# A recurrent four-layer kernel on one Trainium2 core: the second layer's input product moved from whole-array matmuls into column tiles of the recurrence's PSUM, and the order of each tile's work rewritten

## The reference

```python
# layer 0: modulated dense layer (ys and d depend on the batch row only)
x = x + einsum('bsi,io->bso', x * ys[:, None, :], weight) * d[:, None, :]
# layer 1: tanh RNN over the 128 steps
h = tanh(h @ Wh + (x @ Wx + b))        # x = x + all h
# layer 2: per row a dense layer, base + a rank-8 product A B made from cond
x = x + (x + x @ (base + A B))
# layer 3: LSTM over the 128 steps
a = x @ Wx + b + h @ Wh                # 512 -> 2048: gates i, f, o, g
c = sigmoid(f) * c + sigmoid(i) * tanh(g); h = sigmoid(o) * tanh(c)   # x = x + all h
```

## Time and profile before

| what | value |
|---|---|
| median of 3 runs | 1139.91 us (1139.41 to 1141.58) |
| the profiled execution | 1140.8 us, its span 1139.0 us |
| instructions | 57838, of them 26364 matmuls |
| TensorE busy | 97% of the span |
| VectorE, ScalarE, GpSimd busy | 80%, 37%, 5% |
| granted TensorE clock, mean | 0.995 |

### The profile page before, as it was taken

How to read it: one execution, slowest core, us unless ns; L and a number is a source line. 1 busy time by engine, 2 the same in 40 slices (tenths; PEclk the granted TensorE clock), 3 DMA queues, 4 the chain that set the end, 5 groups by cost and what they waited for, 6 DMA issues and landing times.

```text
span 1139.0 us, 57838 instructions
## 1 busy us (share of the span) xinstructions
PE 1099.2 (97%) x26364; PEld 744.4 (65%) x26364; DVE 908.3 (80%) x2726; ACT 426.1 (37%) x1034; POOL 55.2 (5%) x75
## 2 busy tenths in 40 slices
PE   5779999999999999999999999999999999999997
PEld 3446656766766676667666666766666676667587
DVE  7898888888878888887788888888888887887766
ACT  6784333333333333333333333333333333333332
POOL 0000000000000000000000000000000000000000
PEclk9899999999999999999999999999999999999999
DMA  9991000000000000000000000000000000000000
GB/s 338 404 369 40 22 22 3 22 22 22 22 22 21 4 22 21 22 22 22 22 14 11 22 22 22 22 22 19 6 22 22 22 22 21 13 3 13 12 14 22
DMA packets 24613, 51.45 MB, mean 45 GB/s; under 512 B 4160, under 2 KB 4288, under 8 KB 23344
## 3 DMA queue, kind: packets, MB, share of 16 engines
q1 hardware_dynamic: 23936, 47.49, 11.8%
q10 hardware_dynamic: 432, 0.26, 0.1%
HBM read 39.36 MB, written 8.39 MB: 42 GB/s over the span
## 4 chain that ended last, share of the span: by engine, by line
PE 83%; DVE 8%; DMA 3%; ACT 2%; issue 1%; SPq 1%; ACTq 0%; DVEq 0%
PE ps_gates L1543 52%; PE ps_l L1474 13%; PE ps_x L1474 7%; PE ps_rnn L1591 7%; DMA ring<-in_hw 3%; PE ps_lr L1474 2%; PE ps_l L1543 2%; DVE gates_ring L1103 1%; SPq L403 1%; PE ps_z L1512 1%; DVE rnn_pre L928 1%; PE ps_gates L1443 1%; DMA rows<-in_ln_b 1%; DVE late L1133 0%; ACT rnn_h L522 0%
## 5 line engine op out<-in xcount | busy, mean ns | idle before, releaser
L1543 PE MATMUL ps_gates<-big,rows 128*32 128x512 f16 (+1 forms) x6144 | 344.4, 372 | 2.1 <-DVE gates_ring L1103 1.3
L1543 PE MATMUL ps_gates<-big,lstm_h 128*32 128x512 f16 (+1 forms) x6144 | 343.8, 372 | 2.1 <-DVE lstm_h L1136 2.0
L1543 PEld LDWEIGHTS ps_gates<-big,rows 128*32 128x32 f16 x6144 | 163.6, 97 | 162.2 <-DVE gates_ring L1103 10.2
L1543 PEld LDWEIGHTS ps_gates<-big,lstm_h 128*32 128x32 f16 x6144 | 160.4, 97 | 148.0 <-DVE lstm_h L1136 3.6
L657 ACT ACTIVATE gates_ring<-gates_ring 128x256 f32<-128x256 f32 x128 | 53.4, 417 | 284.0 <-DVE gates_ring L1103 284.0
L1103 DVE SCALAR_TENSOR_TENSOR gates_ring<-ps_gates,tile_un,rows 128x256 f32<-128x256 f32 x248 | 108.8, 479 | 37.6 <-PE ps_gates L1543 37.6
L1591 PE MATMUL ps_rnn<-wh_hi,rnn_h 128*32 128x128 f16 x4096 | 103.4, 221 | 1.3 <-ACT rnn_h L522 0.7
L1133 DVE SCALAR_TENSOR_TENSOR late<-gates_ring,tile_g,cell_tanh 128x128 f16<-128x128 f32 x127 | 44.7, 352 | 60.2 <-ACT cell_tanh L666 60.2
L1591 PEld LDWEIGHTS ps_rnn<-wh_hi,rnn_h 128*32 128x32 f16 x4096 | 72.0, 97 | 26.3 <-issue 4.4
L1474 PE MATMUL ps_l<-xs,w_hi 128*128 128x128 f16 x1024 | 79.5, 221 | 1.6 <-DVE xs L837 1.6
L1474 PE MATMUL ps_l<-x,wx_hi 128*128 128x128 f16 x1024 | 78.1, 219 | 1.5 <-DVE x L837 1.5
(11 more groups left out here) (201 smaller groups left out, 1596.0 us busy)
## 6 DMA issues: line engine op xcount, KB each, us to landing
ring<-in_hw SPq DMA_DIRECT2D x16, 1024.0 KB, 15.0
xT_sb<-in_xT SPq DMA_DIRECT2D x32, 256.0 KB, 2.8
outT<-late SPq DMA_DIRECT2D x32, 256.0 KB, 2.0
big<-in_wx SPq DMA_DIRECT2D x5, 1024.0 KB, 14.4
big<-in_wh SPq DMA_DIRECT2D x5, 1024.0 KB, 14.7
big<-in_w SPq DMA_DIRECT2D x1, 1024.0 KB, 5.4
big<-in_hw SPq DMA_DIRECT2D x1, 1024.0 KB, 13.7
late<-in_base SPq DMA_DIRECT2D x1, 1024.0 KB, 14.7
```

Source lines behind the costliest of these rows:

```text
L1543: last = nc.tensor.matmul(by_chunk_of_gate(bank[B * j:B * j + B, columns]), of_step, tile_columns(w, j)[:, gates], start=start, stop=stop, ...
```

## The change

- `l1` is no longer a dense product of a tile. `l1(r)` makes x @ Wx of one step in 48 column-tiled matmuls of 128 moving columns, straight into the bank in which `rnn(r)` then goes on summing. The RNN uses two banks in turn for this (`ps_hidden` = `ps_rnn`, `ps_l1`). `l1(r+1)` stands right behind `rnn(r)`.
- For that the two products need one scale: the scale of the hidden state becomes one per tile (`tile_h`, `tile_cap`, `tile_hidden`, `rnn_scale`), some more operations on single columns. `xw1` and `xw1T` are gone; `rnn_sums` adds the bias, with the tile's factor. `x1_16` has two buffers.
- On TensorE, `l0`, all of `x3_base` and `x3_low_rank` stand in one block behind `lstm(t)`, `rnn(r)`, `l1(r+1)` and `z`. Parts of `gates_x` are placed around `lstm(t+2)` and `lstm(t+3)`.
- On VectorE, `lstm_cell` comes right behind `lstm_sums`, before `rnn_sums`; `x3_first` moves to the first step of a tile and `x3_low` to the second, and `xs` moves from GpSimd to VectorE. ScalarE's order follows.
- The body for tile 31 is reordered in the same way, with `x2` at its end, and the first LATE `gates_x` waits for the last `rnn_sums`.

```diff
-        x1_16 = sb("x1_16", [P, 2, KC, TOK], fp16)
+        x1_16 = [sb(f"x1_16_{q}", [P, 2, KC, TOK], fp16) for q in range(2)]
+        ps_hidden = [ps_rnn, ps_l1]
@@ gpsimd, loop
                 spread_x(0, 1)
-                xs(i + 2)
@@ vector
+            def tile_cap(c, n):
+                linked(nc.vector.tensor_scalar(tile_s[:, c:c + n, 1:2], tile_s[:, c:c + n, 1:2], x1_cap[:], None, ALU.min))
+            def tile_hidden(c, n):
+                nc.vector.tensor_scalar(tile_h[:, c:c + n], tile_s[:, c:c + n, 1:2], rnn_link[:], None, ALU.mult)\
+                  .then_inc(tile_h_ready, n)
-            def xw1(c):
...
             def rnn_sums(r):
-                i, s = r // STEPS, r % STEPS
+                i = r // STEPS
                 dve.wait_ge(rnn_ps, r + 1)
-                if s == 0:
-                    dve.wait_ge(xw1_ready, i + 1)
-                nc.vector.transpose(rnn_turned[:], by_chunk(ps_rnn[:, 0:P])).then_inc(rnn_turned_ready, 1)
+                nc.vector.transpose(rnn_turned[:], by_chunk(ps_hidden[r % 2][:, 0:P])).then_inc(rnn_turned_ready, 1)
                 dve.wait_ge(rnn_turned_ready, r + 1)
-                nc.vector.scalar_tensor_tensor(rnn_pre[:], rnn_turned[:], un_rnn[:], xw1T[:, :, s],
+                nc.vector.scalar_tensor_tensor(rnn_pre[:], rnn_turned[:], tile_s[:, i, 4:5],
+                                               b1T_sb[:].unsqueeze(2).broadcast_to([P, KC, B]),
                                                ALU.mult, ALU.add).then_inc(rnn_pre_ready, 1)
@@ vector, loop
                 lstm_sums(t)
                 if i == LAG:
                     xs_low(c)
-                    xw1(LAG)
+                lstm_cell(t)
                 rnn_sums(r)
-                lstm_cell(t)
                 lstm_turned(t)
+                mask_z(a1)
                 rnn_out(r)
-                mask_z(a1)
                 zm_low(a1)
                 lstm_out(t)
...
+                x1(c)
+                x3_first(a1)
+                x1_low(c)
+                lstm_sums(t + 1)
+                lstm_cell(t + 1)
+                rnn_sums(r + 1)
+                lstm_turned(t + 1)
+                rnn_out(r + 1)
                 lstm_out(t + 1)
+                x3_low(a1)
+                if in_l0(i + 1):
                     tile_scales(i + 2, 1, 0)
                     tile_undo(i + 2, 1, 0)
+                    xs(i + 2)
@@ tensor
-            def gates_x(t):
+            def gates_x(t, thirds=(0, 1, 2)):
                 x16, at = x3_16[t // STEPS % 2], B * (t % STEPS)
-                wait(pe, gates_ready, sums_before(t - 1))
-                if t == LATE:
-                    pe.wait_ge(l0_scaled, TILES)
-                    pe.wait_ge(xw1_ready, TILES)
+                if thirds[0] == 0:
+                    wait(pe, gates_ready, sums_before(t - 1))
+                    if t == LATE:
+                        pe.wait_ge(l0_scaled, TILES)
+                        pe.wait_ge(rnn_turned_ready, T)
...
+            def hidden_products(r, x, w, start, stop):
+                for j in range(KC):
+                    last = nc.tensor.matmul(by_chunk(ps_hidden[r % 2][B * j:B * j + B, 0:P]), x, hidden_columns(w, j),
+                                            start=start, stop=stop, tile_position=(0, B * j))
+                return last
+
+            def l1(r):
+                i, at = r // STEPS, B * (r % STEPS)
+                if r % STEPS == 0:
+                    pe.wait_ge(x1_lo_ready, i + 1)
+                wait(pe, rnn_turned_ready, r - 1)
+                for n, (part, w) in enumerate(((0, wx1_hi), (0, wx1_lo), (1, wx1_hi))):
+                    for k in range(KC):
+                        hidden_products(r, x1_16[i % 2][:, part, k, at:at + B], w[:, k], n == 0 and k == 0, False)
@@ tensor, loop
                 lstm(t)
                 rnn(r)
+                l1(r + 1)
                 z(a1)
-                if in_l0(i):
-                    l0(c)
-                x3_base(a1, (0, 1))
+                l0(c)
+                x3_base(a1, range(KC))
+                x3_low_rank(a1)
+                lstm(t + 1)
                 rnn(r + 1)
-                lstm(t + 1)
+                l1(r + 2)
                 gates_x(t + 2)
-                gates_x(t + 3)
+                gates_x(t + 3, (0,))
                 lstm(t + 2)
+                gates_x(t + 3, (1, 2))
                 rnn(r + 2)
-                x3_base(a1, (2, 3))
-                x3_low_rank(a1)
-                if in_l0(i):
-                    l1(c)
+                l1(r + 3)
+                gates_x(t + 4, (0, 1))
+                lstm(t + 3)
+                gates_x(t + 4, (2,))
                 rnn(r + 3)
-                lstm(t + 3)
-                gates_x(t + 4)
-                if in_rnn(i + 1):
-                    gates_x(t + 5)
+                l1(r + 4)
+                gates_x(t + 5)
```

More of the change, by code:

```diff
@@ L792, in _ @@
                 zm_high(a1)
+                low_rank_share(a1)
+                x3_high(a1)
                 lstm(t + 1)
@@ L1240, in _ @@
             dve.wait_ge(ld_b1, 16)
-            xw1(0)
             tile_undo(1, XT_RING - 2, 1)
@@ L1264, in _ @@
             x2(0)
-            xw1(1)
             rnn_sums(4)
@@ L1346, in _ @@
                 lstm_out(t + 2)
-                x3_first(a1)
-                x3_low(a1)
+                gate_scales(i)
+                if in_l0(i + 1):
+                    xs_low(i + 2)
+                if i + 3 < TILES:
+                    dve.wait_ge(m_spread, i + 3)
+                    x_magnitude(i + 3, 0)
+                lstm_sums(t + 3)
+                lstm_cell(t + 3)
                 rnn_sums(r + 3)
-                if in_l0(i):
-                    xw1(c)
+                lstm_turned(t + 3)
                 rnn_out(r + 3)
-                lstm_gates(t + 3)
                 lstm_out(t + 3)
@@ L1496, in l0 @@
                 dense(ps_l0, w0_hi, w0_lo, xs16, range(KC)).then_inc(l0_ps, 1)
-            def l1(c, outs=range(KC)):
-                if outs[0] == 0:
-                    pe.wait_ge(x1_lo_ready, c + 1)
-                    wait(pe, xw1_ready, c)
-                last = dense(ps_l1, wx1_hi, wx1_lo, x1_16, outs)
-                if outs[-1] == KC - 1:
-                    last.then_inc(xw1_ps, 1)
             def z(a):
@@ L1589, in rnn @@
                     for k in range(KC):
-                        for j in range(KC):
-                            last = nc.tensor.matmul(by_chunk(ps_rnn[B * j:B * j + B, 0:P]), rnn_h16[:, part, k],
-                                                    hidden_columns(w[:, k], j), start=(n == 0 and k == 0),
-                                                    stop=(n == 2 and k == KC - 1), tile_position=(0, B * j))
+                        last = hidden_products(r, rnn_h16[:, part, k], w[:, k], False, n == 2 and k == KC - 1)
                 last.then_inc(rnn_ps, 1)
@@ L1693, in _ @@
                 rnn(r)
+                l1(r + 1)
                 z(a1)
-                x3_base(a1, (0, 1))
+                x3_base(a1, range(KC))
+                x3_low_rank(a1)
                 lstm(t + 1)
                 rnn(r + 1)
+                l1(r + 2)
                 gates_x(t + 2)
+                lstm(t + 2)
                 gates_x(t + 3)
-                lstm(t + 2)
                 rnn(r + 2)
-                x3_base(a1, (2, 3))
-                x3_low_rank(a1)
+                l1(r + 3)
                 lstm(t + 3)
+                rnn(r + 3)
                 gates_x(t + 4)
-                rnn(r + 3)
             for t in range(T - LAG * STEPS, T):
```

184 lines of the change are left out of this document (87 added, 97 removed).

## The result

The changed kernel takes 1153.26 us (median of 4 runs, 1152.42 to 1154.13), the kernel before 1140.49 beside it (1139.41 to 1141.58): a ratio of 1.0108, 95% interval 1.0096 to 1.012. The forecast was 1141.3, with 1131 to 1151 as its range. The profiled execution has a span of 1150.9 us, 11.9 more than before.

A forecast was written before the change was run, and what follows sets the result against it. TensorE, busy 97% of the span, was taken to bound the kernel. Span 1139.0 - 9.5 (loop) + 0 (ahead of it) + 2.9 (tile 31 and end) + 8 (instruction supply) = 1140.4; the median lies 0.9 above: 1141.3 us, range 1131 to 1151.

The forecast's parts named there:

- Ahead of the loop: Before the loop: 2 us less l1 work, but TensorE waits for the weight buffers' DMA (ring); 0, bounds -2 and +1.
- `l1` in column tiles: TensorE, each tile: four steps of 0.67, 2.68 us against 2.68 for the dense product without its switch; no gain or loss.
- The one block: TensorE in the loop: two changes of kind per tile instead of four, saving 0.20 us, 33.00 to 32.80.
- The waits of the earlier trace: TensorE in the loop: waits of gates_x(t + 3) for VectorE's gates in some tiles go.
- rival 3: VectorE late in a tile's first step: each tile loses 0.6, 17 us in all, 1150 to 1158; chance 0.17.
- rival 4: TensorE: short weight loads bind in runs of 96 or more pairs, l1 costs double, 78 us more, 1212; chance 0.02.
- The supply in the loop: TensorE at rnn, l1, z: late instruction packets cost 0.8 us in about one tile in three, 8 us; bounds 0 and 17.
- rival 2: TensorE's instruction supply keeps up, without gaps: 1133.3 us (1131 to 1136); chance 0.26.
- a: Tile 31: x3_low_rank waits 0.5 us for zm_low, since l0 no longer covers it.
- c: Tile 31: gates_x(120) waits 1.7 us for the last rnn_sums.
- b: Tile 31: rnn(126) stands behind a whole gates_x, a wait of 1.0 us.
- What came behind: After tile 31's lstm steps: z(31)'s gap of 1.04 us taken as half, and 0.1 for a switch.

The follow-up runs named there:

- e10_short_l1: e9_all with l1(1) to l1(7), ahead of the loop, cut to the product of the high parts, 16 pairs each instead of 48: 1133.99 us.
- e9_all: Changed kernel plus e3_both's two edits, l1(0) ahead of l0(1), and e8_tail's order of tile 31: 1135.93 us, ratio 0.9968 to the kernel before.
- e4_before_lib: The kernel before with one tiny unread GpSimd reduction (128x1) at the very end of GpSimd's program: 1142.81 us, ratio 1.0017 to the kernel before.
- e1_lib_back: The changed kernel with one tiny unread GpSimd product (128x1) at the very end of GpSimd's program: 1146.04 us, ratio 1.0048 to the kernel before.
- e3_both: The changed kernel with the edits of e1_lib_back and e2_l1_moved together: 1138.99 us, ratio 0.9985 to the kernel before.
- e2_l1_moved: The changed kernel with l1(r+1) of a tile's first step moved in the loop behind x3_low_rank: 1145.19 us, ratio 1.0038 to the kernel before.
- e5_before_zz: The kernel before with z's 48 column-tiled pairs issued twice, the second set overwriting the first: 1169.94 us.
- e8_tail: e3_both with rnn(126) and l1(127) ahead of gates_x(119), and rnn(127) ahead of lstm(119), in tile 31: 1137.43 us, ratio 0.9976 to the kernel before.

## Why the prediction was wrong

**The step that failed is "Ahead of the loop", taken at 0 with bounds of -2 and +1. It measured +10.2** (+10.8 by `z`, with the 0.67 of `l1` in front of it). The argument was that TensorE waits there for the ring until 74.74, so that nothing small could count. It went wrong in two ways.

First, it followed only the engines and lines that the change edits in the head, and forgot that taking `xs` off GpSimd changes what GpSimd executes last, and first of the next execution. The trace of before had the rows for it: 10.4 and 7.2 us of "issue" at GpSimd's changes of kind. I had counted the removal of GpSimd's `xs` only as relief for VectorE. This part is 6.4 of the 10.2 us (113.21 to 106.82), 7.2 in the time.

Second, it priced the supply of instructions in the loop and not in the head. The change puts 9 steps of 48 pairs there for 3 dense tiles of 48: 288 pairs more, over two packets. With the DMA full each takes 6.2 us, and the ring's waits, on which the 0 rested, were used up by it. What e10_short_l1 takes off e9_all directly is 1.4 us, work included; more of the price is that the late `ident` had nowhere left to hide (it costs 2.1 us in the kernel before, by e4_before_lib, and 7.2 in the changed one, by e1_lib_back). From e1_lib_back to e3_both the head is 0.2 us less late, and from there to e9_all (105.95 to 105.07) 0.9, by a mere change of order on TensorE, which also moves where its packets end.

A third cost is not separated from these two: the clock. The order of the head changed too, and TensorE is granted 1.2 GHz for 17.0 us ahead of the loop in the changed kernel, for 10.2 in the kernel before and in e1_lib_back, and for 6.8 in e9_all. Where TensorE's work is on the chain, half clock for 6.8 us more is up to 3.4 us. The forecast had no term for it. The last 1.2 us (103.63 against 102.38) aren't settled.

**What held.** `l1` in column tiles at 0.67 a step. The one block: 33.00 to 32.76 in a quiet tile, against 32.80. The waits of the earlier trace rows gone. No wait for VectorE's hidden state in the loop, so rival 3 didn't come, nor did rival 4. The supply in the loop: gaps in ten tiles, as "one tile in three" had it; e2_l1_moved takes them away and e5_before_zz puts them into the kernel before. Their sum, 8.6 against 8, agrees better than its parts, and that is luck: the gaps are 0.62 us on average, not 0.8, and the rest is small delays that no row names, in the same tiles and in seven others. The Trainium skill ("Runtime: NRT & Kernel Launch", Instruction fetch mechanics) calls the crossing of a block mostly hidden; here it agrees with the 128 pairs of a packet and disagrees with the gaps, which rival 2 would have needed absent. The prediction's "two in store" is what that section says of the instruction memory in general; for TensorE it gives 2048 instructions, which would be eight packets, and the gaps of e5_before_zz behind runs of 144 short pairs don't agree with so large a store.

Tile 31: from its `lstm(116)` to `lstm(120)` are 1098.29 - 1067.90 = 30.4 us, against 30.3, with a and c at 0.5 and 1.8; e8_tail got 1.6 of b and c back by order alone. What came behind was taken at -0.7 and measured +0.2: the issue gap in `z(31)` was counted as half gone, but it is 0.83 where it was 1.04, and one of 0.26 stands ahead of it. So the end is +3.8 against +2.9, inside its bounds.

With the head as it measured, the sum would have been 1140.4 + 10.2 = 1150.6, against a span of 1150.9; that it comes so near is in part luck, the end 0.9 above and the loop 0.6 below their terms. The range was too narrow by one step: the head's bounds came from six small operations, not from asking which other resources the stage shares.

## What to carry to other kernels

Read GpSimd's "issue" before each change of kind of operation, and look at what it runs last and first: taking an operation off it, far from the start, moved the start's select by 10.4 us here and cost 7.2. Count short pairs of weight load and matmul in packets of 128, keep runs of them apart with slower products, and count again, at a higher price, where the DMA is full. A wait that hides a cost is used up once: when two parts of a change rest on the same wait, only one of them is free. And compare two kernels at a mark that has the same work in front of it in both.

## What was not expected of the hardware

- What GpSimd ran last in one execution decides the start of the next: 0.35 us ahead of the first select where the program ends with a product (ten kernels), and 10.4, 10.8 and 12.2 where it ends with a reduction (e4_before_lib, the changed kernel, e2_l1_moved). That it is the loading of code is my reading of the "issue" rows.
- A packet of instructions comes about every 6.2 us while the other queues move 384 GB/s; a gap from it ends at the same time even when TensorE comes 1.6 us earlier. In the changed kernel's loop, with the DMA nearly idle, 3.3 us is the least between two.
- 48 pairs with 0.4 us of work made the loop 3.0 us later there, in the profiled execution. Over its seven runs the time is 1.1 to 6.0 us above the kernel before's median, more at a lower granted clock.
